# First attention: which queue issues the stores of rounded keys and queries

## The reference

```python
def _L0_xattn_ref(qk, v, masks, Wq, bq, Wk, bk, Wv, bv, Wo, bo):
    ...
    q = jnp.einsum('ed,bdw->bew', Wq, qp) + bq[:, None]
    k = jnp.einsum('ed,bdw->bew', Wk, qp) + bk[:, None]
    val = jnp.einsum('ed,bdw->bew', Wv, vp) + bv[:, None]
    ...
    scores = jnp.einsum('bhdi,bhdj->bhij', qh, kh) / jnp.sqrt(jnp.asarray(dh, qh.dtype))
    scores = jnp.where(mp[:, :, None, :] > 0, scores, jnp.asarray(-1000000000.0, scores.dtype))
    attn = jax.nn.softmax(scores, axis=-1)
    o = jnp.einsum('bhij,bhdj->bhdi', attn, vh).reshape(BN, DK, W)
    o = jax.nn.gelu(o, approximate=False)
    out = jnp.einsum('de,bew->bdw', Wo, o) + bo[:, None]
```

## Time and profile before

| | |
|---|---|
| median of 3 runs | 1108.44 us (1107.95 to 1110.77) |
| profiled execution, its own time | 1100.67 us |
| its span, first to last instruction | 1098.9 us |
| busy share of the span | PE 86%, DVE 62%, ACT 41%, POOL 34% |
| mean granted TensorE clock | 0.926 |
| TensorE first starts the scores of the attention | 28.35 us |
| last step of the attention's loop on ScalarE | 135.13 us |

### The profile page before, as it was taken

One profiled execution on the slowest core, in us unless ns is written; L12 is line 12 of the kernel. 1 busy time (PEld: TensorE's weight loads), 2 busy tenths in 40 slices (PEclk: granted clock), 3 DMA queues, 4 the chain that ended last, 5 costly groups with the idle time before them and its releaser, 6 DMA issues. The chain is left out here.

```text
span 1098.9 us, 14895 instructions
## 1 busy us (share of the span) xinstructions
PE 941.0 (86%) x4891; PEld 610.1 (56%) x4891; DVE 683.1 (62%) x1143; ACT 447.4 (41%) x656; POOL 374.4 (34%) x362
## 2 busy tenths in 40 slices
PE   2788786989999899999877598899986689679997
PEld 0566623756666566663445344455473455457886
DVE  2566464686687687764858753566644887445334
ACT  0255413325656566652234422344403555235130
POOL 5552021224566565651222220211220222048431
PEclk9999855999999999999889699799988999879999
DMA  6766103146977967556304100000003100032001
GB/s 158 230 169 175 63 0 140 39 164 243 342 266 269 372 202 267 201 177 216 115 23 160 39 0 1 20 1 1 1 0 153 49 0 1 5 92 77 29 10 38
DMA packets 41237, 124.00 MB, mean 113 GB/s; under 512 B 5313, under 2 KB 5761, under 8 KB 38473
## 3 DMA queue, kind: packets, MB, share of 16 engines
q1 hardware_dynamic: 33640, 98.41, 26.7%
q0 software_dynamic: 7520, 24.65, 6.8%
HBM read 137.19 MB, written 23.59 MB: 146 GB/s over the span
## 5 line engine op out<-in xcount | busy, mean ns | idle before, releaser
L1275 POOL DMA_INDIRECT f_picks<-f_turn_xn,f_target x47 | 106.7, 2271 | 78.9 <-ACT f_turn_xn L1164 78.0
L1691 PE MATMUL banks<-f_t_dn,f_z 128*128 128x512 f32 x188 | 88.5, 593 | 0.6 <-issue 0.6
L1419 DVE TENSOR_TENSOR f_gu_lo<-f_t_gu,f_gu_hi 128x2048 fp32r<-128x2048 f32 x24 | 55.1, 2296 | 18.1 <-ACT f_gu_hi L1150 15.2
L1269 POOL DMA_INDIRECT f_turn_xn<-f_xn_rows,f_token x47 | 48.5, 1033 | 46.0 <-DVE f_token L1413 18.7
L1419 DVE TENSOR_TENSOR f_xn_lo<-f_t_gu,f_xn_hi 128x2048 fp32r<-128x2048 f32 x23 | 52.8, 2297 | 17.5 <-ACT f_xn_hi L1150 17.5
L628 DVE TENSOR_REDUCE a_mx<-banks 128x8 f32<-128x1024 f32 x32 | 39.2, 1226 | 27.1 <-PE banks L723 27.1
L2389 ACT ACTIVATE a_e<-banks 128x1024 f32<-128x1024 f32 x32 | 32.8, 1025 | 54.1 <-PE banks L2481 54.1
L2419 DVE TENSOR_REDUCE a_mx<-banks 128x8 f32<-128x1024 f32 x32 | 39.1, 1223 | 21.8 <-PE banks L2461 21.8
L1150 ACT CAST f_gu_hi<-f_t_gu 128x2048 fp32r x24 | 45.7, 1904 | 13.4 <-DMA f_t_gu<-in_f_gu 11.2
L1150 ACT CAST f_xn_hi<-f_t_gu 128x2048 fp32r x23 | 43.8, 1903 | 13.3 <-DMA f_t_gu<-in_f_gu 9.9
L1157 ACT ACTIVATE f_sil<-banks 128x256 f32<-128x256 f32 x47 | 18.1, 384 | 75.9 <-PE banks L255 75.9
(11 more groups left out here) (414 smaller groups left out, 2567.6 us busy)
## 6 DMA issues: line engine op xcount, KB each, us to landing
f_t_gu<-in_f_gu SPq DMA_DIRECT2D x47, 1024.0 KB
f_t_dn<-in_f_dn SPq DMA_DIRECT2D x47, 512.0 KB
f_t_gu<-f_picks SPq DMA_DIRECT2D x8, 1024.0 KB, 5.2
a_st<-a_parts SPq DMA_DIRECT2D x32, 208.0 KB
f_xn_rows<-f_turn_xn SPq DMA_DIRECT2D x9, 256.0 KB, 2.1
x_res<-in_x SPq DMA_DIRECT2D x8, 256.0 KB, 5.6
a_out_mask<-in_mask SPq DMA_DIRECT2D x8, 256.0 KB, 6.1
a_parts<-a_qk_hi SPq DMA_DIRECT2D x8, 256.0 KB
```

Source lines behind the costliest of these rows:

```text
L1269: pool.indirect_dma_start(t_rows[:, t % F0_BUFS, :], None, dram["f0_xn_rows"], bass.IndirectOffsetOnAxis(ap=token[:, t:t + 1], axis=0))\
L1275: pool.indirect_dma_start(dram["f0_picks_flat"], bass.IndirectOffsetOnAxis(ap=target[:, t:t + 1], axis=0), t_y[:, t % F0_BUFS, :], None).t ...
L1419: dve.tensor_tensor(t_gu_lo[t % 2], t_gu[:, bass.ds(i, 1), :, :].rearrange("p i c n -> p (i c n)"), t_gu_hi[t % 2].bitcast(F32), ALU.subtr ...
L1691: mm = pe.matmul(ps[:, TY_BANK + t % 2, :], t_zt[:, t % 2, c, :], t_dn[:, t % F0_BUFS, c, :], start=c == 0, stop=c == F0_IC - 1)
```

## The change

The five stores of a batch are issued by ScalarE, no more by SyncE. The three of `qk_hi` follow the cast that makes it; the two of `qk_lo` come at the end of the iteration, behind the exponential of unit u's even half (for batches 0 to 2, before the loop, right behind the first three). Each waits for its part's semaphore. SyncE keeps the loads, the rows that are fixed, and the stacked reads; its wait for `fixed_stored` now comes right behind the issue of the fixed rows.

```diff
-                    def store(b):
-                        qs, ks = slice(0, A0_HEADS), slice(A0_HEADS, 2 * A0_HEADS)
-                        sp.wait_ge(qk_hi_ready, b + 1)
-                        hi, lo = qk_hi[:, b % 2, :].bitcast(F32), qk_lo[:, b % 2, :].bitcast(F32)
-                        sp.dma_start(part_of(b, slice(0, 2 * A0_HEADS), 0), hi).then_inc(parts_stored[b % 2], 16)
-                        sp.dma_start(part_of(b, qs, 1), hi[0:A0_DK]).then_inc(parts_stored[b % 2], 16)
-                        sp.dma_start(part_of(b, ks, 2), hi[A0_DK:P]).then_inc(parts_stored[b % 2], 16)
-                        sp.wait_ge(qk_lo_ready, b + 1)
-                        sp.dma_start(part_of(b, qs, 2), lo[0:A0_DK]).then_inc(parts_stored[b % 2], 16)
-                        sp.dma_start(part_of(b, ks, 1), lo[A0_DK:P]).then_inc(parts_stored[b % 2], 16)
...
-                    store(0)
                     sp.wait_ge(fixed_stored, 16 * 3)
                     load_mask(1)
                     load_mask(2)
                     load_ctx(0)
                     fetch(0)
                     load_x(3)
-                    store(1)
                     load_x(4)
                     load_ctx(1)
                     fetch(1)
                     load_mask(3)
-                    store(2)
                     load_x(5)
...
                         load_ctx(b)
-                        store(b)
                         fetch(b)
...
+                    def store_upper(b):
+                        hi = qk_hi[:, b % 2, :].bitcast(F32)
+                        act.wait_ge(qk_hi_ready, b + 1)
+                        act.dma_start(part_of(b, slice(0, 2 * A0_HEADS), 0), hi).then_inc(parts_stored[b % 2], 16)
+                        act.dma_start(part_of(b, qs, 1), hi[0:A0_DK]).then_inc(parts_stored[b % 2], 16)
+                        act.dma_start(part_of(b, ks, 2), hi[A0_DK:P]).then_inc(parts_stored[b % 2], 16)
+
+                    def store_lower(b):
+                        lo = qk_lo[:, b % 2, :].bitcast(F32)
+                        act.wait_ge(qk_lo_ready, b + 1)
+                        act.dma_start(part_of(b, qs, 2), lo[0:A0_DK]).then_inc(parts_stored[b % 2], 16)
+                        act.dma_start(part_of(b, ks, 1), lo[A0_DK:P]).then_inc(parts_stored[b % 2], 16)
...
                     for b in range(A0_EARLY):
                         upper_part(b)
+                        store_upper(b)
+                        store_lower(b)
                     take_values(0)
                     for u in range(UNITS + 1):
                         if u >= 1:
                             exponent(2 * u - 1)
                         if batch_at(u) is not None:
                             upper_part(batch_at(u))
+                            store_upper(batch_at(u))
                         if values_at(u) is not None:
                             take_values(values_at(u))
                         if u >= 1:
                             take_out(u - 1)
                         if u < UNITS:
                             exponent(2 * u)
+                        if batch_at(u) is not None:
+                            store_lower(batch_at(u))
```

More of the change, by code:

```diff
@@ L400, in load_mask @@
                           .then_inc(mask_loaded[b], 16)
-                    def part_of(b, jobs, part):
-                        return parts[b, jobs, part * A0_DH:(part + 1) * A0_DH, :]
                     def same(row):
                         return row.unsqueeze(1).broadcast_to([B, A0_HEADS, row.shape[1]])
-                    def store(b):
-                        qs, ks = slice(0, A0_HEADS), slice(A0_HEADS, 2 * A0_HEADS)
-                        sp.wait_ge(qk_hi_ready, b + 1)
-                        hi, lo = qk_hi[:, b % 2, :].bitcast(F32), qk_lo[:, b % 2, :].bitcast(F32)
-                        sp.dma_start(part_of(b, slice(0, 2 * A0_HEADS), 0), hi).then_inc(parts_stored[b % 2], 16)
-                        sp.dma_start(part_of(b, qs, 1), hi[0:A0_DK]).then_inc(parts_stored[b % 2], 16)
-                        sp.dma_start(part_of(b, ks, 2), hi[A0_DK:P]).then_inc(parts_stored[b % 2], 16)
-                        sp.wait_ge(qk_lo_ready, b + 1)
-                        sp.dma_start(part_of(b, qs, 2), lo[0:A0_DK]).then_inc(parts_stored[b % 2], 16)
-                        sp.dma_start(part_of(b, ks, 1), lo[A0_DK:P]).then_inc(parts_stored[b % 2], 16)
                     def fetch(b):
@@ L541, in upper_part, with part_of @@
                         act.copy(qk_hi[:, b % 2, :], qk[:, b % 2, :]).then_inc(qk_hi_ready, 1)
+                    def part_of(b, jobs, part):
+                        return dram["a0_parts"][b, jobs, part * A0_DH:(part + 1) * A0_DH, :]
+                    qs, ks = slice(0, A0_HEADS), slice(A0_HEADS, 2 * A0_HEADS)
+                    def store_upper(b):
[9 more added lines that the diff above has]
+                        act.dma_start(part_of(b, ks, 1), lo[A0_DK:P]).then_inc(parts_stored[b % 2], 16)
                     def take_values(b):
```

## The result

The change makes the kernel slower: the median goes from 1108.20 us (1106.48 to 1110.77, 4 runs) to 1131.89 us (1127.93 to 1132.60, 4 runs), a ratio of 1.0205 with a 95% interval of 1.0174 to 1.0235. That is 23.7 us, where 8.1 were forecast and the range ended at 1122. Ratios leave disturbed runs out, so they can differ a little from the quotient of the medians.

A forecast was written before the change was run, and what follows sets the result against it. In the attention's loop no engine is full; a circle of short steps on three engines sets the time. 7.1 - 0.9 + 1.9 - 2.8 + 2.8 = 8.1 us on 1108.44 gave 1116.5, range 1109 to 1122.

The forecast's parts named there:

- Issues ahead of the copy: Iterations 1, 3, 5, 7, 9: three store issues on ScalarE delay the outputs' copy; 1.5 us each, 1.1 in iteration 1, sum 7.1.
- the first rival: Rival: issues on ScalarE are nearly free, passed while the copy is under way; 1104.7 us, faster; chance 0.1.
- The two lower issues at nothing: Two lower-part store issues fall in ScalarE's 1.28 us of idle time ahead of the odd exponential; cost nothing.
- Start, 0.9 gained: At the start, batch 1's mask leaves SyncE's queue earlier without stores ahead; 0.9 us gained, bounds 3.3 gained and 1.0 lost.
- Batch 3's mask, 1.9: Store 2, under way when the read ahead of this mask starts, delays mask and iteration 1 by 1.9 us; bounds 0 and 3.7.
- The third rival: Rival: stores overtake loads; mask 3 late by the full 3.7 us, mask 4 keeps its 2.8 us stall; 1121.1; chance 0.12.
- The second rival: Rival: TensorE's clock does not fall and batch 3's mask is not delayed; about 1111.3 us; chance 0.18.
- Batch 4's mask, 2.8 gained: Store 2 leaves earlier, so this mask no longer comes late and iteration 3's stall goes; 2.8 us gained, bounds 0 and 2.8.
- The clock, 2.8: The new gap ahead of the turned outputs lowers TensorE's clock in four iterations, 0.7 us each, 2.8 us.
- The upper bound of 3.8 us: Most that TensorE's clock falls could cost: 0.94 us of the projection in each of four iterations.

The follow-up runs named there:

- the gap filled: Changed kernel plus ten identity turns on TensorE ahead of the turned outputs in iterations 1, 3, 5, 7 and 9: 1113.95 us, 1.0028 of before.
- the copies: Kernel before plus four unread ScalarE copies between cast and copy of outputs in iterations 1, 3, 5, 7, 9: 1133.03 us, 1.0221; with ten TensorE turns 1103.79 us, 0.9970.
- the ten turns of 2.39 us: Changed kernel plus identity turns on TensorE, ten ahead of turned outputs in iterations 1 to 9 (odd), six in 11, 13, 15: 1102.75 us, 0.9931 of before.

## Why the prediction was wrong

*Issues ahead of the copy: right.* Forecast 1.5 us for an iteration, measured 1.36 with the clock held. An issue on ScalarE costs what it cost on SyncE. Nearly free issues, the first rival, fell: they are free only where no wait stands ahead of them. The upper bound was taken from the first store's issue of 2.02 us; the next one in the same trace, at 11.95, took 2.54.

*The two lower issues at nothing: right,* and for a better reason than the idle time: they run beside the compute part.

*Start, 0.9 gained: wrong, 0.* The mask of batch 1 leaves at 16.89, and the scores start as late as before.

*Batch 3's mask, 1.9: too low.* GpSimd starts 3.8 us later, just past the upper bound of 3.7. Iteration 1 is 4.6 us longer, so 0.8 are left for its issues, forecast at 1.1. The third rival had this delay right, whether for its reason stays open; its second half, that batch 4's mask would be late too, did not come. The second rival, in which the clock does not fall and the mask is not delayed, fell on both counts.

*Batch 4's mask, 2.8 gained: right in kind.* With the stores behind the exponentials or the gap filled, iteration 3 has lost its stall.

*The clock, 2.8: the step that failed.* I had the mechanism and the place, and booked it as four single falls of 0.7 us each, by the fall of iteration 3 in the trace before. There it came in a loop that filled itself up again: one stall, then dense iterations. With a gap in every second iteration the clock came back only for two short stretches between 56 and 138 us (86.8 to 90.2 and 100.4 to 103.9), and every iteration from 2 to 10, the even ones too, ran at 7.7 to 10 us. The windows, of two long stretches of the changed kernel:

```profile
56.10:86.70 30.60, 29.04 (x290) 21.21 (x284) 15.48 (x23) 10.82 (x14) 10.16 (x9) 0.50 0.49 128
104.00:137.90 33.90, 30.73 (x309) 23.88 (x310) 14.29 (x21) 12.54 (x17) 4.39 (x3) 0.50 0.38 98
```

TensorE is busy 29.0 of 30.6 us there, because it works at half speed, and still is not granted the full clock. What the term is worth: change 1.0205 against 1.0028 with the gap filled is 1.8%, 19 to 20 us of the 23.7 (by the two intervals, give or take 5); in the traces iterations 1 to 10 give 21.8 us for it, 90.3 less 68.5. So the clock term was mis-sized sevenfold.

The other terms add up to 5.3 us. Measured they are 6.2 for the issues (four by 1.36 and 0.8), 0 for the start, 3.8 and -2.8 for the masks, 7.2 in all; the ten iterations with the gap filled are 7.3 us longer than before. The sum without the clock was 2 us too low, and that it was no worse is in part luck, since the errors have both signs.

The upper bound of 3.8 us was none: it priced one matmul at two levels of the clock, not an iteration. The iterations themselves would have given it, 9 iterations by the 2.9 us between 8.3 and 5.45, but only the trace after has iterations wholly at half clock. A warning stood in the trace before, though. Its clock also fell at 116.2 us, in iteration 13, with no late mask and no long stall; TensorE had waited 1.18 us for the exponential, as it does in each of the late odd iterations (1.19, 1.18 and 1.12 us), less than the 1.9 us that the forecast gave the new gap:

```profile
116.01 1.81 PE L753 MATMUL banks<-a_e,a_v 128*32 128x128 f32 x32 [1.18 <-ACT a_e L557]
```

That iteration took 6.64 us, 1.2 more than its neighbours, and so one fall by itself cost more than the 0.94 us of the bound.

Issues slower on ScalarE than on SyncE had no part in the loss: of those in the loop one, in iteration 7, took 1.53 us and no other over 0.6.

## What to carry to other kernels

A DMA issue of this size cost the issuing engine 0.6 us in the loop, and it is free behind a long instruction but not behind a wait for the engine's own result: put it behind work that is already dispatched. In a loop of small matmuls ask first how idle TensorE becomes in each repetition: a delay of 1.4 us in every second iteration cost 24 us here, and matmuls that compute nothing, put into the gaps, took 18 of them back. Price a loss of clock by whole iterations, not by the matmul at which it begins. And compare a profiled execution with its median first: the one of the kernel before, 7.5 us below it, had five late iterations at 28.0 us that took 33 to 38 in all the other traces with nothing added there.

## What the runs showed of the hardware that was not expected

- Work added on TensorE makes the kernel faster where it holds the clock: 0.9878 on the kernel before, 1.0205 to 1.0028 on the change, 1.0221 to 0.9970 on the copies.
- With a gap once per two iterations the clock is granted at 0.50 for stretches of 30 us in which TensorE's matmuls fill 29 us; being busy at half speed did not bring the full clock back (the ends of matmuls are modelled by the profile, so busy is an upper figure).
- The granted clock doesn't show every matmul at half speed. In iteration 1 of both kernels the projection takes 2.07 or 2.08 us in place of 1.13, and it reads 1.00 all the while; so it does around the ten turns of 2.39 us above. The duration of a known matmul is the surer sign:

```profile
44.68:46.70 2.02, 2.02 (x4) 0.52 (x4) 0.00 (x0) 0.00 (x0) 0.00 (x0) 1.00 0.75 193
...
44.68 2.08 PE L694 MATMUL banks<-a_xn,raw 128*128 128x512 f32 x2 [1.85 <-POOL a_xn L496]
```

- The issuing part of ScalarE runs ahead of its compute part: an issue that stands behind the even exponential in the program began at 87.42, ahead of that exponential's start at 87.79. So an engine's strict order, as told of the kernel before, held here for each of the two parts, and not between an issue and a step ahead of it that is already on its way.
- With stores on a second queue, SyncE's issue of a stacked read took 2.33 in place of 1.59 us and that of a mask 1.27 in place of 0.37, and the mask's work on GpSimd began 3.8 us later. What of this is the sharing of the DMA engines and what the order within the queue was tried only by moving the mask, which removed it; the sharing by itself stays open.
